# A transformer block sandwich on one core: sample loops written out, the output bias back on VectorE in stage two, three stack transfers per slot

## What is computed

```python
x = L0_attn_x                                     # 16 samples x 256 tokens x 128 features
x = x + _layernorm(_L0_attn_ref(_layernorm(x), w_qkv, w_out, b_out))
x = x + _layernorm(_L0_ffn_ref(_layernorm(x), ...))

def _L0_ffn_ref(x, ...):                          # two layers
    for l in range(L):
        x = x + _attn(_ln(x, ln1_w[l], ln1_b[l]), wq[l], wk[l], wv[l], wo[l], bq[l], bk[l], bv[l], bo[l])
        h = _ln(x, ln2_w[l], ln2_b[l])
        moe = _token_moe if l % 2 == 0 else _seq_moe
        x = x + moe(h, gate_w[l], gate_b[l], e_w1[l], e_b1[l], e_w2[l], e_b2[l])
    return x
```

## Time and profile before

| | us |
|---|---|
| median of 3 runs | 1223.89 (1222.18 to 1230.21) |
| the profiled execution: its own time | 1225.62 |
| its span, first to last instruction | 1223.5 |
| PE busy | 1048.5 |
| DVE busy | 952.9 |
| ACT busy | 787.7 |
| POOL busy | 705.1 |

### The profile page before, as it was taken

How to read it: one execution, slowest core, us unless ns; L and a number is a source line. 1 busy time by engine, 2 the same in 40 slices (tenths; PEclk the granted TensorE clock), 3 DMA queues, 4 the chain that set the end, 5 groups by cost and what they waited for, 6 DMA issues and landing times. The chain is left out here.

```text
span 1223.5 us, 38411 instructions
## 1 busy us (share of the span) xinstructions
PE 1048.5 (86%) x10358; PEld 789.4 (65%) x10453; DVE 952.9 (78%) x2887; ACT 787.7 (64%) x1908; POOL 705.1 (58%) x1050
## 2 busy tenths in 40 slices
PE   1899999999999899999379998388989889989997
PEld 1566666666666666666279998255655656658986
DVE  3789999999998999999636654378788888866665
ACT  1677777777777777777158776266766667754554
POOL 3455556566667788777723332677677777533232
PEclk9999999999999999999679999599999999989999
DMA  5442111112112222221122222244222222200000
GB/s 145 110 116 60 51 48 44 48 45 53 51 49 58 57 63 57 59 64 46 45 62 69 70 69 72 65 122 118 63 56 53 62 53 57 52 4 14 19 18 21
DMA packets 120359, 73.10 MB, mean 60 GB/s; under 512 B 10688, under 2 KB 115264, under 8 KB 120256
## 3 DMA queue, kind: packets, MB, share of 16 engines
q1 hardware_dynamic: 101600, 53.12, 16.1%
q10 hardware_dynamic: 14560, 10.35, 3.1%
q0 software_dynamic: 4096, 8.40, 2.3%
HBM read 21.68 MB, written 11.60 MB: 27 GB/s over the span
## 5 line engine op out<-in xcount | busy, mean ns | idle before, releaser
L624 DVE TENSOR_REDUCE negm<-bank 128x2 f32<-128x512 f32 (+1 forms) x576 | 389.2, 679 | 60.7 <-PE bank L315 42.4
L511 ACT ACTIVATE prob<-bank 128x512 f32<-128x512 f32 x576 | 339.3, 595 | 110.2 <-PE bank L337 70.4
L906 POOL TENSOR_SCALAR_AFFINE_SELECT prob<-prob 128x512 f32<-128x512 f32 x384 | 246.5, 645 | 151.7 <-ACT prob L511 149.7
L356 PE MATMUL bank<-prob,vaug 128*32 128x256 f32 (+1 forms) x3072 | 168.4, 338 | 5.2 <-ACT oT L517 3.2
L1239 POOL COPY w_job<-w_s 128x512 f32 x104 | 66.5, 640 | 156.4 <-PE bank L1208 155.3
L323 PE MATMUL bank<-stack 126*128 126x256 bf16 x768 | 149.6, 276 | 0.0
L342 PE MATMUL bank<-stack 128*128 128x256 bf16 x768 | 148.7, 274 | 0.9 <-ACT prob L511 0.9
L1219 PE MATMUL bank<-w_job,prob 128*128 128x128 f32 x1088 | 139.6, 276 | 2.1 <-issue 1.8
L1230 ACT ACTIVATE prob<-bank,b_job 128x128 f32<-128x128 f32 (+1 forms) x416 | 131.6, 400 | 7.5 <-PE bank L1208 5.6
L1219 PEld LDWEIGHTS bank<-w_job,prob 128*128 128x128 f32 x1088 | 132.1, 193 | 5.7 <-issue 3.4
L356 PEld LDWEIGHTS bank<-prob,vaug 128*32 128x32 f32 x3072 | 81.9, 110 | 81.0 <-issue 49.3
(11 more groups left out here) (182 smaller groups left out, 2081.2 us busy)
## 6 DMA issues: line engine op xcount, KB each, us to landing
stack<-parts SPq DMA_DIRECT2D x576, 64.0 KB
w_s<-e_w ACTq DMA_DIRECT2D x32, 256.0 KB, 2.9
oT<-x_routed SPq DMA_DIRECT2D x72, 64.0 KB, 1.7
y_routed<-oT SPq DMA_DIRECT2D x36, 128.0 KB, 1.9
stack<-mT SPq DMA_DIRECT2D x192, 4.0 KB
out<-x_all SPq DMA_DIRECT2D x16, 128.0 KB, 1.8
b_all<-e_b ACTq DMA_DIRECT2D x2, 512.0 KB, 8.4
x_routed<-hk,x_at POOLq DMA_INDIRECT x64, 2.3
```

Of the source, the lines that this page charges most:

```text
L356: m = nc.tensor.matmul(o, w, (prob0, prob1)[kb][:, g % 2, h], start=kb == 0, stop=kb == 1, skip_group_check=True)
L511: nc.scalar.activation(o, s, ACT.Exp, scale=SCALE).then_inc(exp_done, 1)
L624: nc.vector.tensor_reduce(o, s, AX.X, ALU.max, negate=True).then_inc(max_done, 1)
L906: nc.gpsimd.affine_select(out=t, in_=t, compare_op=ALU.is_ge, fill=0.0, base=0, pattern=[[0, HG], [1, P]], channel_multiplier=-1).then_inc ...
```

## The change

Four edits. The loops over steps are gone, and every step is written out. In stage two DVE adds bank and bias into `att` and then `att` to `f_all`, with a wait between; POOL adds the bias only in stage three, and `biased` is counted from there. Placing: piece 3 moves from slot 2 to the front of slot 3, piece 4 from the end of slot 2 and piece 5 from the front of slot 3 to the end of slot 3. The stack: term 0 of the first half goes in slot 1 as soon as `qkf_sb` allows, terms 1 and 3 behind the wait for two counts of `split`, terms 4, 2 and 5 in slot 2; the second half 0, 1, 3 in slot 3 and 4, 2, 5 in slot 0 of the next step.

```diff
             at = lo - (3 if hi == 3 * B else 2)
-            for phase in range(lo // B, hi // B):
-
-                first, last = phase * B + (6 if phase == 1 else 4), phase * B + B - (4 if phase == 2 else 2)
-                peeled(at, first)
-                with eng.Fori(first, last - 1, 2) as n:
-                    for d in range(2):
-                        for k in range(NG):
-                            slot((n + d, d, phase, lo, hi), k)
-                at = last
             if hi == 3 * B:
                 peeled(at, hi)
...
         def dve_residual(i):
 
+            base = NRES * i.v
             dve.wait_ge(o3_ps, i.v + 1)
-            if i.phase > 0:
-                dve.wait_ge(biased, i.v - B + 1)
+            if i.phase == 2:
+                dve.wait_ge(biased, i.v - 2 * B + 1)
                 nc.vector.tensor_tensor(pair(f_all, i), post_bank[:, 0:T].rearrange("p (j d) -> p j d", j=2),
                                         pair(f_all, i), ALU.add).then_inc(res, 2)
                 return
             nc.vector.tensor_tensor(att[:, i.par], post_bank[:, 0:T].rearrange("p (j d) -> p j d", j=2),
                                     bo_s[:, i.phase:i.phase + 1].to_broadcast([P, 2, P]),
                                     ALU.add).then_inc(res, 1)
+            if i.phase > 0:
+                dve.wait_ge(res, base + 1)
+                nc.vector.tensor_tensor(pair(f_all, i), pair(f_all, i), att[:, i.par], ALU.add).then_inc(res, 1)
...
             if k == 3 and placing:
-                dve_place(first, 5)
+                dve_place(first, 3)
             if cur:
                 dve_reduce(cur, k, 1)
...
-            if k == 2 and placing:
-                dve_place(first, 3)
...
-            if k == 2 and placing:
-                dve_place(first, 4)
             if k == 2 and ranked:
                 dve_top(oldest, 0)
             if k == 3 and ranked:
                 dve_top(oldest, 2)
+            if k == 3 and placing:
+                dve_place(first, 4)
+            if k == 3 and placing:
+                dve_place(first, 5)
...
-            if k == 3 and nxt and nxt.phase > 0:
+            if k == 3 and nxt and nxt.phase == 2:
                 pool_bias(nxt)
...
             if half == 0:
-                sp.wait_ge(split, NSPLIT * i.v + (NSPLIT - 1 if 0 in terms else NSPLIT))
+                if 0 in terms:
+                    sp.wait_ge(qkf_sb, 4 * i.v + 4)
+                else:
+                    sp.wait_ge(split, NSPLIT * i.v + (NSPLIT if 2 in terms else NSPLIT - 1))
...
             if k == 1 and nxt:
-                sp_stack(nxt, 0, EARLY_TERMS)
+                sp_stack(nxt, 0, (0,))
+                sp_stack(nxt, 0, (1, 3))
             if k == 2 and nxt:
-                sp_stack(nxt, 0, LATE_TERMS)
+                sp_stack(nxt, 0, (4, 2, 5))
             if k == 3 and nxt:
-                sp_stack(nxt, 1, EARLY_TERMS)
+                sp_stack(nxt, 1, (0, 1, 3))
             if k == 0 and cur:
-                sp_stack(cur, 1, LATE_TERMS)
+                sp_stack(cur, 1, (4, 2, 5))
```

More of the change, by code:

```diff
@@ L996, in pool_slot @@
                 nc.gpsimd.tensor_copy(hk[:, oldest.par], hn[:, oldest.par]).then_inc(hk_sb, 1)
-        EARLY_TERMS, LATE_TERMS = (0, 1, 3, 4), (2, 5)
         def term_rows(t):
```

## The result

The changed kernel took 1205.41 us in the median of four executions (1204.16 to 1207.01), the kernel before beside it 1224.39 (1222.18 to 1230.21). That is a ratio of 0.984, with a 95% interval of 0.980 to 0.988. The forecast was 1218 with a range of 1202 to 1234; the time lies in it, 12.6 us under the forecast and beside rival (a), 1206. The profiled execution took 1206.4 with a span of 1204.6, 18.9 under the span of before.

What follows compares the result with a forecast made beforehand. PE was taken as the bound, with DVE beside it in the attention stages. Terms -4.6, +5.7, -8.1 and +1 for fetching gave -6.0: 1219.6 from the profiled 1225.62, which stood 1.7 over the median, hence 1218 us, range 1202 to 1234.

Steps and rivals of the forecast that it cites:

- (a): Rival: DVE gets the lock favourably, stage two even, no stall of fetched adds in stage three; 1206 us, chance 0.26.
- Stage one: Steps 4 to 13: written out instead of looped, each saves 0.46 us, -4.6 us in all.
- Stage two: Bias and placing cost 0.45 us on each of 16 steps, +7.3, less 1.6 for the loops: +5.7 us.
- The bank's new gap: Stage two: PE's next group of maxima waits for the late reduction's bank, 0.3 to 0.65 us of new gap.
- the transposes' gap: Stage two: PE's wait for the cast before the transposes grows from 0.81 to 1.05 to 1.2 us.
- the gap at the end of the step: Stage two: PE's 0.59 us behind the cast of `expert_all` shrinks, taken as 0.25 us off a step.
- Stage three: Steps 36 to 43 give -5.1 us, steps 34 and 35 give -3; together -8 us.
- the price of such a step: Steps 36 to 43: three steps with stalled fetched adds at 19.7 us each, the other five at 17.5.
- The likeliest case: Whole kernel: the forecast itself, 1218 us, own range 1210 to 1225, chance 0.41.
- (b): Rival: in stage two six steps fall to the lower clock, +12 us; 1230 us, chance 0.17.
- (c): Rival: the clock falls in every step from 18 to 29, 24 us; 1242 us, chance 0.09.
- (d): Rival: the loops' cost is not in the loops, or fetching eats the gain; 1224 us, chance 0.07.

Runs made afterwards that it cites:

- e1: The kernel before with only the loops over steps written out; 1213.32 us, ratio 0.990.
- e3: The kernel before with only the placing edit; 1226.58 us, ratio 1.002.
- e2: The kernel before with only the bias edit of stage two; 1231.24 us, ratio 1.005.
- e10: The changed kernel with the loops over steps put back, all other edits kept; 1217.42 us, ratio 0.994.
- e11: The changed kernel executed a second time, nothing altered; 1205.03 us, ratio 0.985 to the kernel before.
- e5: The changed kernel with the bias of stage two back on POOL; 1200.28 us, ratio 0.976 to the kernel before.
- e4: The kernel before with only the stack transfer edit; 1217.63 us, ratio 0.993.
- e7: The changed kernel with DVE's second pair of fetched adds moved from slot 1 to slot 0; 1212.6 us, ratio 0.988 to the kernel before.

## Why the prediction was right, and where not

**Stage one: right.** -4.6 was predicted from the two rows of stretches and -4.6 measured; the kernels that are written out show -4.2 to -4.6. For fetching 1 us was allowed. Steps 14 and 16 took 16.89 and 16.92 us instead of 16.6, +0.6 in all, and step 14 took 16.9 in every written-out kernel and in no looped one. But PE's waits in these steps are those of before, and no run shows that it is the fetching.

**Stage two: the sign was wrong.** +5.7 was predicted and -0.9 measured. What DVE does was seen as foretold: the add held behind `rest` (at least 1.0 said, 1.40 measured), the cast behind it free, `expert_all` under 0.3. The terms that failed are PE's gaps. The bank's new gap is 0.40 (0.3 to 0.65 said), but the transposes' gap did not grow to 1.05 to 1.2: it is 0.78. DVE's lateness of 1.4 us replaced the cast's stall of 1 us and did not come on top of it. That is 0.37 us a step instead of 0.7. And the gap at the end of the step (0.59 in step 25, 0.41 in the mean of the eight) went wholly, where I took 0.25 of it. The prediction had no term for the new gap of 0.27. With it PE's waits in the eight steps rise by 1.2 us (10.3 to 11.5), while the stretch falls by 1.5, so the waits do not account for the gain: it stands in PE's busy time (130.9 to 129.1 us at a clock of 1.00 in both), whose ends are modelled, and its cause stays open.

Two readings of the trace of before were off as well. The 0.67 us taken as the new add's floor is 0.42 to 0.46. And the cast of `expert_all` (474.26 to 475.36) began after the bias had ended and lasted through the send and until POOL's copy to `hk` had ended:

```profile
474.93 0.41 POOL L996 COPY hk<-hn 128x256 f32<-128x256 f32 x1
```

It is free in e1 and in e3, with the bias still on POOL. What the prediction gave to the bias's leaving is therefore not shown to be its work. The row with which it called the trace in agreement with the Trainium skill is also that of a cast, which has one SBUF input; operations with two are the pair of fetched adds and the new add.

In the looped kernel the bias alone cost 0.47 a step (e2) and the placing alone gave 0.21 (e3), both with the sign that was said (0.7 and 0.25), but in e2 PE paid at the end of the step and not at the maxima. Together with the stack order the two, +0.26 in sum, became -0.30 a step (e10); the stack order alone gave nothing there (142.57 against 142.62). Written out, the change's steps are 0.1 us longer than looped, where the prediction took 0.2 off for the writing out. Adding terms priced one by one was the error: the edits act on the same two engines' order of arrival.

**Stage three: right mechanism, too small a size.** -8 was predicted and -13.5 measured, -14.8 in the second execution. Steps 34 and 35 gave 4.2 instead of 3: the row's waits fell from 4.6 to 0.8, the waits for the reduction rose by 1.1, and step 35's fall of the clock, which the prediction had as a perhaps, went. For steps 36 to 43 the prediction said that the written-out steps remove the stall and that the earlier row may bring it back. The runs bear out both: written out alone -9.3 (9.9 said at most), the stack transfers alone +0.6, though there it is another operation that is held. The pairs of 1.89 us came in three steps of eight, 37, 39 and 43, as foretold; before they were five. The term of wrong size is the price of such a step. It was put at 19.7 with a fall of the clock, and they cost 18.42 to 18.49 without one, 3.7 us less in the three; that is most of the 4.3 us between -5.1 and -9.4. In the second execution (e11) four of the eight pairs lasted 1.51 and one 1.90, the steps were 17.3 to 18.3 us, and the stretch was 1.0 us shorter.

**The number.** The likeliest case, 1210 to 1225, was missed. The time is inside 1202 to 1234 because that range was widened to take in (a), and the misses of stage two (6.6 us) and of stage three (5.5) both went the same way.

**The rivals.** (a) came nearest, partly by luck. Its even stage two is what happened; its other ground, no stall of the fetched adds, held in e1 and not in the change, where only the clock's part of the price went. (b) and (c): no step from 18 to 31 left 1.00 in the change, nor with the bias alone; the one kernel in which some did was e1, without the bias, where gaps of 1.46 and 1.48 us were followed by steps at 0.92. (d) is refuted by stage one and by e10: writing out is worth 9 to 13 us of span here (1223.5 against 1212.0; 1213.3 against 1204.6 and 1200.5), 4.4 to 4.6 of them as plain time in stage one.

**Open.** The rows of the first steps and of the jobs, -1.9 and +3.0, vary by about as much between executions of one kernel. Ten profiled executions with the new stack order took 96.7 to 99.7 us to step 4 and four without it 98.9 to 99.9, so part of the -1.9 may be the stack's; that was not settled. Which of placing and stack order steadies the written-out stage two (143.6 in e1, 138.2 in e5) was not tried apart.

## What to carry to other kernels

Where a profile shows small DVE operations that last several times their shortest, look up which GpSimd operation ends just before they do, and how many hundredths of a microsecond lie between the two starts. Any edit that moves either engine, even one that only drops register work, deals these meetings anew, so price edits together and not one by one, and expect a stretch of steps to jump by 0.5 to 3 us a step. If DVE needs an operation beside such work, let one of its inputs come from a bank: here steps with such an add were 0.58 us shorter, of which up to 0.12 may be the wait that went with it.

## What the runs showed of the hardware

- A gap of PE does not decide the clock by its length alone. In steps 36 to 43 of before, gaps of 1.62 us were followed by a granted clock of 0.91 in four steps, and one of 1.63 by none (step 43, 18.30 us); in e3 one of 1.62 by none (step 36, 18.34 us) and one of 1.63 by 0.84 (step 41, 20.94); in e10 a gap of 2.57 came with 0.92 in step 37 (21.02 us) and one of 2.58 with 1.00 in step 39 (20.38). No gap up to 1.38 was followed by a fall in steps 36 to 43 of before, the change, e1, e4, e10 and e11. Elsewhere falls came with gaps between the two: 1.46 us in step 25 of e1 with 0.92 in the step behind it, 1.56 in step 45 of e7 with 0.91.
- A small DVE operation can stay held through an indirect transfer's issue on POOL and the operation queued behind it. The subtraction of 128x8, 0.17 us when free, began 0.33 us behind the start of a DMA_INDIRECT and lasted through it and through `rest`, 1.85 us (e10): it did not get in between the two. But not every operation that falls into such an issue is held. The same subtraction, begun 0.24 us behind one (step 35 of e4, 843.68 against 843.44), ran in 0.17 us, and the change's add of two SBUF tiles, begun 0.28 us behind one (583.55 against 583.27), in 0.42. What parts these cases is not known.
- The changed kernel's two profiled executions agree to 0.02 us in each of steps 22 to 29, and differ by up to 1.4 us in stage three (step 45: 18.61 and 17.22), where DVE waits for fetched rows.
